# A three-layer GRU on graphs and a routed feed-forward on one Trainium2 core: the gated groups routed and placed in pairs

## The chip, the cores and the metric

The kernel runs on one core of one Trainium2 chip. Its five engines each follow their own list of instructions and wait for each other on semaphores: TensorE (PE; PEld are its weight loads), VectorE (DVE), ScalarE (ACT), GpSimd (POOL) and SyncE (SP). Transfers run beside them on 16 DMA engines. The metric is the device time of one execution in microseconds (us), lower is better.

## The reference

```python
A = (adj != 0)                              # 64 graphs of 128 nodes, 128 channels
h = layernorm(x)
for i in range(3):                          # GRU on the graph
    m = h @ weight[i];  aggr = A^T m
    h = gru_cell(aggr, h, w_ih, w_hh, b_ih, b_hh)
x = x + h
xf = layernorm(x)                           # 8192 tokens
H = gelu(xf @ W1 + b1)                      # 128 -> 512, exact gelu
probs = softmax(H @ Wg + bg)                # 8 experts
assign = argmax(probs)
out = x + probs[assign] * (H @ Wd[assign] + bd[assign])
```

## The kernel before, in words

The 64 graphs are 16 groups of four (512 columns). Every order is written out by hand: each engine has its own block with the same step numbers.

**Opening and GRU steps.** 48 units (four groups in flight, three layers each), one per step. A unit needs its rows in a high and a low half, since a product of fp32 precision is made of three matmuls (`three`, L481 to L483). For units of the first layer VectorE makes the low half of unit 0 (L1026), GpSimd that of all others (`first_rows_low`, L363), and TensorE's `neighbours` (L517, L518) waits for it.

**Gate steps** (`gate_step` on each engine, s = 0 to 18). For group s TensorE transposes the rows (`turned`, L607, one step ahead), makes the hidden layer in four chunks in four banks (`hidden`), which ScalarE empties with gelu (L907); for group s-1 it makes the gate's logits (L650). VectorE *routes* group s-2: it turns the logits (L1179), finds the winning expert and writes a one-hot tile `oh`. TensorE counts with five small matmuls into bank `pF` how many earlier tokens chose each expert (the *ranks*, L668, L671), semaphore `g_rk`. VectorE *places* group s-3: from the ranks and a running `base` it makes the row number of each token (`pos`, last instruction L1222), and the softmax gives its probability. GpSimd waits for both, then sends the group's four graphs of 128 rows by four indirect DMAs to the buffer `sorted_rows` in HBM, sorted by expert (L448). TensorE's four hidden banks are one set, so the next group's chunk waits for ScalarE's gelu of the last, and that for TensorE's signal `g_w1`.

**Tables.** After the ranks of eight groups VectorE computes which expert each of the first 24 slots of 128 rows has (`full_blocks_counted`, `full_blocks_placed`). `table(1)`, after TensorE's step 11, turns that by matmuls into one row of bank `pT`, VectorE copies it to `tables` (`tabled`, L1263, semaphore `tab_ok`), and TensorE's next transposes, which write `pT` too, wait for it. `table(2)` does the same for the rest, among the expert steps.

**Expert steps.** 18 slot groups (71 slots): SyncE loads sorted rows, TensorE makes the hidden layer again and the product with the slot's expert (L712), VectorE adds bias, multiplies by the probability and adds the residual (L1374, L1378), GpSimd scatters each slot's rows to the output (L459). After steps 9, 12 and 15 GpSimd drains its queue (`RETIRE`, L475). The last three slot groups use three banks in turn (`YB`).

## Time and profile before

| | us |
|---|---|
| median of 3 runs | 567.49 (566.56 to 571.98) |
| the profiled execution, its own time | 569.5 |
| its span | 567.8 |
| TensorE / weight loads busy | 511.8 / 418.8 |
| VectorE / ScalarE / GpSimd busy | 370.2 / 331.4 / 376.9 |
| mean granted clock of TensorE | 0.947 |

A step of the GRU and a gate step follow each other closely on TensorE; from about 288 us on the program is in the gate steps, from about 412 us in the expert steps. "remote" or "another core or an unknown queue" as a releaser means that the profile does not show what the engine waited for; "issue" that the engine itself was late.

### The profile page before, as it was taken

Reading aid. Unit: us, or ns where it says so; the run is one execution under the profiler, and the core shown is the slowest. Engines: PE = TensorE matmul, PEld = TensorE weight load, DVE = VectorE, ACT = ScalarE, POOL = GpSimd, SP = SyncE. Lnnn points to the kernel's source line nnn. Section 1 sums busy time; section 2 is a strip of 40 time slices with the busy share of each in tenths; the row PEclk is TensorE's granted clock in tenths of the full one; section 3 lists DMA queues with packets and bytes.
Section 4 is the critical chain, followed back from the end, with each engine's and each line's share of the span. In section 5 each row is a group of like instructions: output and inputs, shape, how many; then the busy total and the mean of one; then the engine's idle time right before and its main releaser. Section 6 shows DMA issues by size and latency. Waiting matters only on the chain.

```text
span 567.8 us, 10433 instructions
## 1 busy us (share of the span) xinstructions
PE 511.8 (90%) x3249; PEld 418.8 (74%) x3249; DVE 370.2 (65%) x1154; ACT 331.4 (58%) x594; POOL 376.9 (66%) x373
## 2 busy tenths in 40 slices
PE   8899999999999999999999689686795999798794
PEld 4678888888888888888877457363584998696684
DVE  5768687798888878897798456454662544353452
ACT  3867986779776897678778357253432442442430
POOL 3579977799798997988756555543555446335545
PEclk9999999999999999999999888787897999799978
DMA  8794000000000000000000111133211322221100
GB/s 224 228 275 119 1 0 1 1 1 2 0 2 1 1 1 2 0 1 0 1 2 15 40 45 35 39 80 81 59 49 62 91 77 81 61 58 45 38 29 21
DMA packets 37317, 26.50 MB, mean 47 GB/s; under 512 B 6140, under 2 KB 33920, under 8 KB 37264
## 3 DMA queue, kind: packets, MB, share of 16 engines
q1 hardware_dynamic: 31344, 16.91, 11.1%
q0 software_dynamic: 4320, 8.53, 4.4%
q8 instruction: 28, 0.46, 0.4%
q10 hardware_dynamic: 1600, 0.40, 0.3%
q14 instruction: 25, 0.20, 0.2%
HBM read 16.69 MB, written 9.59 MB: 46 GB/s over the span
## 4 chain that ended last, share of the span: by engine, by line
PE 76%; issue 7%; DVE 5%; another core or an unknown queue 4%; ACT 3%; POOL 3%; DMA 1%; POOLq 1%; DVEq 0%; ACTq 0%
PE bank L481 17%; PE bank L483 17%; PE bank L482 16%; PE bank L712 8%; PE bank L518 4%; PE bank L504 3%; PE bank L517 3%; PE bank L650 3%; ACT adj_i L907 2%; POOL out_dram L459 2%; PE bank L607 1%; PE bank L698 1%; PE bank L567 1%; DMA xrow<-in_x_dram 1%
## 5 line engine op out<-in xcount | busy, mean ns | idle before, releaser
L907 ACT ACTIVATE adj_i<-bank,b1c 128x512 f32<-128x512 f32 (+1 forms) x136 | 88.4, 686 | 139.3 <-PE bank L483 84.3
L459 POOL DMA_INDIRECT out_dram<-cand,home x71 | 70.3, 991 | 69.5 <-DVE cand L1378 40.8
L448 POOL DMA_INDIRECT sorted_rows<-xrow,pos x64 | 62.0, 968 | 57.5 <-issue 49.9
L369 POOL TENSOR_TENSOR diff<-hT,n_sb 128x512 f32<-128x512 f32 x48 | 76.4, 1592 | 11.4 <-ACT n_sb L814 11.4
L712 PE MATMUL bank<-wd_sb,adj_i 128*128 x568 | 71.1, 283 | 8.3 <-issue 8.3
L712 PEld LDWEIGHTS bank<-wd_sb,adj_i 128*128 128x128 f32 x568 | 69.0, 199 | 9.2 <-issue 9.1
L481 PE MATMUL bank<-hT_hi,w_hi 128*128 128x512 f32 (+1 forms) x136 | 63.1, 464 | 5.4 <-issue 3.0
L371 POOL TENSOR_TENSOR diff<-z_sb,diff 128x512 f32<-128x512 f32 x48 | 63.4, 1321 | 3.8
L481 PE MATMUL bank<-ag_hi,wf_hi 128*128 128x512 f32 x144 | 61.0, 423 | 0.2 <-DVE ag_lo L1064 0.2
L481 PE MATMUL bank<-hT_hi,whh_hi 128*128 128x512 f32 x144 | 59.5, 413 | 0.6 <-issue 0.6
L483 PE MATMUL bank<-hT_hi,w_lo 128*128 128x512 f32 (+1 forms) x136 | 58.2, 428 | 1.5 <-issue 1.4
L482 PE MATMUL bank<-hT_lo,w_hi 128*128 128x512 f32 (+1 forms) x136 | 58.0, 427 | 1.2 <-issue 1.0
L483 PE MATMUL bank<-hT_hi,whh_lo 128*128 128x512 f32 x144 | 57.9, 402 | 0.0
L482 PE MATMUL bank<-hT_lo,whh_hi 128*128 128x512 f32 x144 | 57.8, 402 | 0.0
L483 PE MATMUL bank<-ag_hi,wf_lo 128*128 128x512 f32 x144 | 57.1, 397 | 0.0
L482 PE MATMUL bank<-ag_lo,wf_hi 128*128 128x512 f32 x144 | 56.7, 394 | 0.0
L388 POOL TENSOR_TENSOR hT_lo<-hT,hT_hi 128x512 fp32r<-128x512 f32 x32 | 41.4, 1294 | 11.7 <-ACT hT_hi L893 11.7
L518 PE MATMUL bank<-A,hn_lo 128*128 128x128 f32 x192 | 45.5, 275 | 0.0
L517 PE MATMUL bank<-A,hn_hi 128*128 128x128 f32 x192 | 43.1, 263 | 1.9 <-POOL hn_lo L363 1.7
L1374 DVE TENSOR_TENSOR r_sb<-bank,bd_bc 128x128 f32<-128x128 f32 x71 | 19.2, 288 | 38.0 <-remote 27.3
L1077 DVE TENSOR_TENSOR hT<-n_sb,diff 128x512 f32<-128x512 f32 x48 | 41.5, 864 | 0.4 <-POOL diff L371 0.4
L1064 DVE TENSOR_TENSOR ag_lo<-bank,ag_hi 128x512 fp32r<-128x512 f32 x48 | 33.0, 687 | 13.3 <-ACT ag_hi L853 13.2
(176 smaller groups left out, 1153.2 us busy)
## 6 DMA issues: line engine op xcount, KB each, us to landing
adj_i<-sorted_rows SPq DMA_DIRECT2D x71, 66.0 KB
xrow<-in_x_dram SPq DMA_DIRECT2D x16, 256.0 KB, 3.7
adj_i<-in_adj_dram SPq DMA_DIRECT2D x16, 256.0 KB, 4.0
out_dram<-cand,home POOLq DMA_INDIRECT x71
sorted_rows<-xrow,pos POOLq DMA_INDIRECT x64
sorted_rows<-padrow SPq DMA_DIRECT2D x9, 66.0 KB
bd_bc<-in_L_ffn_bd_dram SPq DMA_DIRECT2D x1, 512.0 KB, 4.4
w1raw<-in_L_ffn_W_dram SPq DMA_DIRECT2D x1, 256.0 KB, 4.3
```

What stands on the lines that cost most here:

```text
L369: nc.gpsimd.tensor_tensor(diff[:, b, :], hT[:, g, :], n_sb[:, b, :], ALU.subtract).then_inc(diff_ok, 1)
L371: nc.gpsimd.tensor_tensor(diff[:, b, :], z_sb[:, g, :], diff[:, b, :], ALU.mult).then_inc(zd_ok, 1)
L448: nc.gpsimd.indirect_dma_start(out=sorted_rows, out_offset=bass.IndirectOffsetOnAxis(ap=pos[:, g, j:j + 1], axis=0), in_=xrow[:, g * GR + ...
L459: nc.gpsimd.indirect_dma_start(out=h_out, out_offset=bass.IndirectOffsetOnAxis(ap=home[:, s - 1, j:j + 1], axis=0), in_=yo[:, b, j, :], in ...
L481: nc.tensor.matmul(o, w_hi, x_hi, start=start, stop=False)
L482: nc.tensor.matmul(o, w_hi, x_lo, start=False, stop=False)
L483: return nc.tensor.matmul(o, w_lo, x_hi, start=False, stop=stop)
L517: nc.tensor.matmul(pAG[:, c], hn_hi[:, u % 2, c], A[:, u % QUAD, c], start=True, stop=False)
L518: last = nc.tensor.matmul(pAG[:, c], hn_lo[:, u % 2, c], A[:, u % QUAD, c], start=False, stop=True)
L712: last = nc.tensor.matmul(o, HT[:, sg % 2, k, j * P:(j + 1) * P], wd_sb[:, bass.ds(at + k * P, P)], start=(k == 0), stop=(k == KC - 1))
L907: nc.scalar.activation(HT[:, hb, k, 0:n], HB[k][:, 0:n], ACT.Gelu, bias=b1c[:, k:k + 1]).then_inc(done, 1)
L1077: tt(hT[:, u % QUAD, :], n_sb[:, u % 2, :], diff[:, u % 2, :], ALU.add).then_inc(h_ok, 1)
```

## The change

Gated groups are handled two at a time. Their tiles are twice as wide (`DUO` = 8 graphs), and one bank of logits holds both groups. VectorE routes a pair at odd steps from 3 on (`routed`), TensorE makes the pair's ranks with nine matmuls at the end of the same step, and VectorE places the pair at the next, even step (`placed`); GpSimd then issues eight scatters in a row. Besides: GpSimd drains after expert steps 6 and 12 instead of 9, 12 and 15; the low half of unit 2 is made by VectorE in its opening step 1, behind its adjacency; the tables go to columns 128 to 511 of the ranks' bank `pF` instead of `pT`, the first one inside TensorE's step 12 behind its transposes, and what waits for the copy is no longer the transposes but the ranks of step 13; the three banks of the last slots are taken in another order.

```diff
-        RETIRE = (9, 12, 15)
+        RETIRE = (6, 12)
+        DVE_LOW = (0, 2)
...
+        def routed(s):
+
+            return (s - 3) // 2 if s % 2 and inside(s - 3, GROUPS) else None
+
+        def placed(s):
+
+            return (s - 4) // 2 if s % 2 == 0 and inside(s - 4, GROUPS) else None
...
                 if s == 1:
                     row_scale(3)
-                    first_rows_low(2)
                     old_state(0)
...
-                g = s - 3
                 if s == 3:
                     row_scales(QUADS - 1)
-                if inside(g, GROUPS):
-
-                    if g == 0:
+                q = placed(s)
+                if q is not None:
+
+                    if q == 0:
                         pool.wait_ge(g_tok, 1)
-                    pool.wait_ge(g_prob, g + 1)
-                    pool.wait_ge(g_pos, g + 1)
+                    pool.wait_ge(g_prob, q + 1)
+                    pool.wait_ge(g_pos, q + 1)
                     settle(pool)
-                    for j in range(GR):
+                    for j in range(DUO):
                         nc.gpsimd.indirect_dma_start(
-                            out=sorted_rows, out_offset=bass.IndirectOffsetOnAxis(ap=pos[:, g, j:j + 1], axis=0),
-                            in_=xrow[:, g * GR + j, :], in_offset=None).then_inc(g_early if g < EARLY else g_late, 16)
+                            out=sorted_rows, out_offset=bass.IndirectOffsetOnAxis(ap=pos[:, q, j:j + 1], axis=0),
+                            in_=xrow[:, q * DUO + j, :], in_offset=None).then_inc(
+                                g_early if q * DUO < EARLY * GR else g_late, 16)
...
-                    pe.wait_ge(x0lo_ok, made("first", u) - 1) if u else pe.wait_ge(x0lo_first, 1)
+                    if u in DVE_LOW:
+                        pe.wait_ge(x0lo_first, DVE_LOW.index(u) + 1)
+                    else:
+                        pe.wait_ge(x0lo_ok, made("first", u) - sum(v < u for v in DVE_LOW))
...
-                if g == EARLY + 5:
-                    pe.wait_ge(tab_ok, 1)
...
+                if s == EARLY + 4:
+                    table(1)
...
-                    hold(pe, g_lgT, s - 2)
+                    pair, half_of = (s - 1) // 2, slice((s - 1) % 2 * P, ((s - 1) % 2 + 1) * P)
+                    hold(pe, g_lgT, pair - 1)
...
+                    pe.wait_ge(g_oh, q + 1)
+                    hold(pe, g_pos, q)
+                    if s == EARLY + 5:
+                        pe.wait_ge(tab_ok, 1)
...
+                    for j in range(1, DUO + 1):
+                        last = nc.tensor.matmul(pF[:, j * E:(DUO + 1) * E], ones[:],
+                                                oh[:, q % 2, 0:DUO + 1 - j, :].rearrange("p g e -> p (g e)"),
+                                                start=False, stop=(j == DUO))
...
+                hold(pe, tab_ok, n - 1)
                 if n == 1:
-                    pe.wait_ge(g_xlo, EARLY + 5)
-                else:
-                    pe.wait_ge(e_xlo, 4)
+                    pe.wait_ge(g_pos, RANKED)
                 for k in range(3):
-                    last = nc.tensor.matmul(pT[0:1, k * P:(k + 1) * P], tab[:, k:k + 1], ident[:],
+                    last = nc.tensor.matmul(TAB[:, k * P:(k + 1) * P], tab[:, k:k + 1], ident[:],
...
-                if sg == 4:
-                    pe.wait_ge(tab_ok, 2)
...
-            YB = (pF, pX, pAG)
+            YB = (pF, pAG, pX)
...
+            def rows_low_early(u):
+                dve.wait_ge(x0hi_ok, made("first", u))
+                tt(hn_lo[:, u % 2, :], xn[:, u % QUAD, :], hn_hi[:, u % 2, :].bitcast(fp32), ALU.subtract).then_inc(x0lo_first, 1)
...
+                    rows_low_early(2)
...
+                if route is not None:
+                    q, b = route, route % 2
+                    lg = lg4[:, b, :, :]
+                    dve.wait_ge(g_lg, 2 * q + 2)
+                    nc.vector.transpose(lgT[:, b, :, :].rearrange("p g c -> p (g c)"), LG[b][:, 0:2 * P]).then_inc(g_lgT, 1)
+                    dve.wait_ge(g_lgT, q + 1)
+                    tt(lg, lgT[:, b, :, 0:E], bg_bc[:].unsqueeze(1).to_broadcast([P, DUO, E]), ALU.add).then_inc(g_lg4, 1)
+                    dve.wait_ge(g_lg4, q + 1)
                     red(mx[:, b, :], lg, AX.X, ALU.max).then_inc(g_dve, 1)
+                    dve.wait_ge(g_dve, q * ROUTE + 1)
+                    tt(sh[:, b, :, :], lg, mx[:, b, :].unsqueeze(2).to_broadcast([P, DUO, E]),
                        ALU.subtract).then_inc(g_sh, 1)
+                    dve.wait_ge(g_sh, q + 1)
                     stt(mt[:, b, :, :], sh[:, b, :, :], 0.0, rev[:], ALU.is_ge, ALU.mult).then_inc(g_dve, 1)
+                    dve.wait_ge(g_dve, q * ROUTE + 2)
+                    red(mv8[:, b, :], mt[:, b, :, :], AX.X, ALU.max).then_inc(g_dve, 1)
+                    dve.wait_ge(g_dve, q * ROUTE + 3)
+                    tt(oh[:, b, 0:DUO, :], mt[:, b, :, :], mv8[:, b, :].unsqueeze(2).to_broadcast([P, DUO, E]),
+                       ALU.is_equal).then_inc(g_oh, 1)
+                if place is not None:
+                    q, d = place, place % 2
+                    dve.wait_ge(g_rk, q + 1)
+                    tt(rk[:, d, :, :], pF[:, 0:DUO * E].rearrange("p (g e) -> p g e", g=DUO),
+                       base[:].unsqueeze(1).to_broadcast([P, DUO, E]), ALU.add).then_inc(g_place, 1)
+                    dve.wait_ge(g_place, q * PLACE + 1)
+                    tt(base[:], pF[:, DUO * E:(DUO + 1) * E], base[:], ALU.add).then_inc(g_base, 1)
+                    tt(rk[:, d, :, :], rk[:, d, :, :], oh[:, d, 0:DUO, :], ALU.mult).then_inc(g_place, 1)
+                    dve.wait_ge(g_place, q * PLACE + 2)
                     red(posf[:, d, :], rk[:, d, :, :], AX.X, ALU.add).then_inc(g_place, 1)
+                    dve.wait_ge(g_place, q * PLACE + 3)
+                    nc.vector.tensor_copy(pos[:, q, :], posf[:, d, :]).then_inc(g_pos, 1)
+                if s == EARLY + 4:
+                    tabled(0, EARLY_SLOTS, 1)
```

VectorE, where a gated group in the middle is routed and the one before it placed; before the change every step has this piece (`lgT` to `oh` route, `rk`, `base`, `posf`, `pos` place, `hT_lo` is the next group's low half):

```order
L1179 STREAM_TRANSPOSE lgT<-bank 128x128
L1188 TENSOR_TENSOR rk<-bank,base 128x32
L1192 TENSOR_TENSOR lg<-lgT,bg_bc 128x32
L1195 TENSOR_REDUCE mx<-lg 128x4
L1201 TENSOR_TENSOR sh<-lg,mx 128x32
L1205 TENSOR_TENSOR base<-bank,base 128x8
L1206 TENSOR_TENSOR rk<-rk,oh 128x32
L1211 SCALAR_TENSOR_TENSOR mt<-sh,rev 128x32
L1214 TENSOR_REDUCE posf<-rk 128x4
L1219 TENSOR_REDUCE mv<-mt 128x4
L1222 CAST pos<-posf 128x4
L1227 TENSOR_TENSOR oh<-mt,mv 128x32
```

VectorE at the same place with the change, the placement of an even step and the routing of the odd step behind it:

```order
L1215 TENSOR_TENSOR rk<-bank,base 128x64
L1218 TENSOR_TENSOR base<-bank,base 128x8
L1219 TENSOR_TENSOR rk<-rk,oh 128x64
L1221 TENSOR_REDUCE posf<-rk 128x8
L1223 CAST pos<-posf 128x8
L1019 TENSOR_TENSOR hT_lo<-bank,hT_hi 128x512
L1014 SCALAR_TENSOR_TENSOR xn<-xrow 128x128 x2
L1197 STREAM_TRANSPOSE lgT<-bank 128x256
L1199 TENSOR_TENSOR lg<-lgT,bg_bc 128x64
L1201 TENSOR_REDUCE mx<-lg 128x8
L1203 TENSOR_TENSOR sh<-lg,mx 128x64
L1206 SCALAR_TENSOR_TENSOR mt<-sh,rev 128x64
```

Placement and routing no longer alternate instruction by instruction; each stands alone in every second step.

TensorE around the first table, before the change (ranks, table, transposes of the next group, its hidden layer):

```order
L668 MATMUL bank<-oh,before 128x40
L671 MATMUL bank<-oh,ones 128x32
L671 MATMUL bank<-oh,ones 128x24
L671 MATMUL bank<-oh,ones 128x16
L671 MATMUL bank<-oh,ones 128x8
L684 MATMUL bank<-ident,tab 1x128 x3
L607 MATMUL bank<-ident,xn 128x128 x4
L481 MATMUL bank<-hT_hi,w_hi 128x512
```

TensorE at the same place with the change:

```order
L687 MATMUL bank<-oh,before 128x72
L690 MATMUL bank<-oh,ones 128x64
L690 MATMUL bank<-oh,ones 128x56
L690 MATMUL bank<-oh,ones 128x48
L690 MATMUL bank<-oh,ones 128x40
L690 MATMUL bank<-oh,ones 128x32
L690 MATMUL bank<-oh,ones 128x24
L690 MATMUL bank<-oh,ones 128x16
L690 MATMUL bank<-oh,ones 128x8
L621 MATMUL bank<-ident,xn 128x128 x4
L702 MATMUL bank<-ident,tab 1x128 x3
L494 MATMUL bank<-hT_hi,w_hi 128x512
```

The table has moved behind the transposes, and one set of nine rank matmuls stands for two sets of five.

## Rows read from the trace of the kernel before

**Rows 1.** The page, part 2: TensorE's granted clock in 40 slices.
```profile
PEclk9999999999999999999999888787897999799978
```

**Rows 2.** The chain of waits, first gated steps: start, duration, engine, tile, line.
```profile
303.79 0.49 PE bank L607 x4
308.42 0.49 PE bank L607 x4
```

**Rows 3.** Timeline of GpSimd, routing scatters: start us, us, instruction, [idle before <-releaser].
```profile
307.33 1.25 POOL L448 DMA_INDIRECT sorted_rows<-xrow,pos  x1 [0.80 <-issue]
...
321.38 0.95 POOL L448 DMA_INDIRECT sorted_rows<-xrow,pos  x1 [3.86 <-issue]
...
327.83 0.96 POOL L448 DMA_INDIRECT sorted_rows<-xrow,pos  x1 [1.71 <-issue]
...
341.97 0.96 POOL L448 DMA_INDIRECT sorted_rows<-xrow,pos  x1 [3.70 <-issue]
...
349.84 0.95 POOL L448 DMA_INDIRECT sorted_rows<-xrow,pos  x1 [3.12 <-issue]
...
363.83 0.96 POOL L448 DMA_INDIRECT sorted_rows<-xrow,pos  x1 [4.10 <-issue]
...
380.65 0.96 POOL L448 DMA_INDIRECT sorted_rows<-xrow,pos  x1 [3.47 <-issue]
...
397.77 0.96 POOL L448 DMA_INDIRECT sorted_rows<-xrow,pos  x1 [7.34 <-DVE pos L1222]
...
405.79 0.96 POOL L448 DMA_INDIRECT sorted_rows<-xrow,pos  x1 [3.17 <-issue]
...
421.29 0.96 POOL L448 DMA_INDIRECT sorted_rows<-xrow,pos  x1 [5.24 <-issue]
```

**Rows 4.** The scatters' line: min/median/max ns, first and last start.
```profile
L448 POOL DMA_INDIRECT sorted_rows<-xrow,pos x64: 952/958/1246, 307.3 to 425.1; - x64
```

**Rows 5.** Timeline of ScalarE around the first long run of scatters.
```profile
309.72 1.33 ACT L907 ACTIVATE adj_i<-bank,b1c 128x512 f32<-128x512 f32 x2 [0.17 <-PE bank L483]
318.97 1.26 ACT L907 ACTIVATE adj_i<-bank,b1c 128x512 f32<-128x512 f32 x2 [7.04 <-remote]
```

**Rows 6.** Windows: busy us (count) of PE, PEld, DVE, ACT, POOL; clock, DMA, GB/s.
```profile
312.00:314.00 2.00, 2.00 (x16) 1.54 (x16) 1.37 (x7) 0.00 (x0) 1.43 (x2) 1.00 0.10 34
```

**Rows 7.** Timeline of TensorE, the transposes behind the first table.
```profile
370.28 0.63 PE L607 MATMUL bank<-ident,xn 128*128 128x128 f32 x4 [3.12 <-DVE tables L1263]
```

**Rows 8.** Timeline of VectorE, the last instruction of a placement.
```profile
379.67 0.17 DVE L1222 CAST pos<-posf 128x4 uint32<-128x4 f32 x1
```

**Rows 9.** Timeline of GpSimd, output scatters of groups 6, 7, 9, 10 and 12.
```profile
466.39 0.98 POOL L459 DMA_INDIRECT out_dram<-cand,home  x1 [2.80 <-DVE cand L1378]
...
473.88 0.98 POOL L459 DMA_INDIRECT out_dram<-cand,home  x1 [2.55 <-DVE cand L1378]
...
491.13 0.98 POOL L459 DMA_INDIRECT out_dram<-cand,home  x1 [7.26 <-DVE cand L1378]
...
505.14 0.98 POOL L459 DMA_INDIRECT out_dram<-cand,home  x1 [9.16 <-issue]
...
518.61 0.98 POOL L459 DMA_INDIRECT out_dram<-cand,home  x1 [3.36 <-DVE cand L1378]
```

**Rows 10.** The drains' line, in the queue of GpSimd: min/median/max ns.
```profile
L475 POOLq DRAIN  x3: 4963/5047/11122, 493.1 to 543.9; - x3
```

**Rows 11.** Timeline of TensorE, unit 2 of the opening.
```profile
25.37 0.30 PE L517 MATMUL bank<-A,hn_hi 128*128 128x128 f32 x1 [1.69 <-POOL hn_lo L363]
```

**Rows 12.** Windows, the same columns as rows 6, behind that wait.
```profile
26.50:29.90 3.40, 3.40 (x9) 2.67 (x9) 1.03 (x3) 3.36 (x7) 1.28 (x1) 0.51 0.73 211
```

**Rows 13.** Timeline of VectorE, unit 0's low half; unit 2's turned rows.
```profile
9.26 0.69 DVE L1026 TENSOR_TENSOR hn_lo<-xn,hn_hi 128x512 fp32r<-128x512 f32 x1 [0.36 <-ACT hn_hi L835]
...
24.89 0.68 DVE L1013 TENSOR_TENSOR hT_lo<-bank,hT_hi 128x512 fp32r<-128x512 f32 x1
```

**Rows 14.** The page, part 3: TensorE's instruction queue (packets, MB, share).
```profile
q8 instruction: 28, 0.46, 0.4%
```

149 lines of the change are left out of this document (46 added, 103 removed).

## The prediction

> **What bounds the kernel now.** I read the page's clock row first. TensorE's granted clock reads 9 in each of the first 22 of 40 slices and falls below that again and again from the 23rd on [rows 1]; 22 slices of 14.2 us are 312 us, early in the gate steps. So the GRU steps are TensorE at its own pace, and the stage the change works in is one where TensorE is not fed.
>
> How far it is not fed comes from two rows of the chain. Two neighbouring gate steps begin their transposes at 303.79 and 308.42 [rows 2]: an undisturbed step takes 4.63. The stage takes much more. GpSimd's scatters of the first gated group begin at 307.33 and those of the sixteenth at 421.29 [rows 3]: 113.96 us for 15 groups, 7.60 a group. Some 3 us a group are lost.
>
> Where they go is in the spacing of GpSimd's scatters. One takes 0.96 [rows 4] and 0.30 more until the next, so 1.265, four take 5.1 and eight 10.1. Since an undisturbed TensorE step (4.63) is shorter than four scatters (5.1), GpSimd falls behind, and the scatters of two groups run into one. The ten rows shown are starts of such runs (one more, of four, at 372.32, is left out): runs of eight begin at 307.33, 327.83, 349.84, 380.65 and 405.79 (in two of them with a gap under 1 us in the middle), runs of four at 321.38, 341.97, 363.83, 372.32 and 397.77.
>
> What a long run does is seen on ScalarE. In the run from 307.33 to 317.5 its last gelu that starts in time is at 309.72; the next starts at 318.97 after 7.04 of waiting on something the profile can't name [rows 5], 1.4 after the run's end. Yet TensorE was busy for all of 312 to 314 [rows 6]. So what ScalarE lacked was the signal of work that TensorE had done: from about 3 us after the start of a run of scatters, TensorE's signals are not seen until about 1 us after its end. A run of four holds them for some 2 to 3 us, which an engine one chunk ahead survives; a run of eight holds them for 8 and starves everybody. This is my reading, not a row; the change tests it, since it makes **every** run one of eight.
>
> **The change part by part.** The sum is made against the profiled execution (569.5, span 567.8); the median of the runs is 567.49, 2.0 less.
>
> *Low half of unit 2.* TensorE waits 1.69 for GpSimd's [rows 11], behind which 3.4 us run at the low clock [rows 12], 1.7 of them lost. VectorE makes the same half in 0.69 [rows 13] behind its adjacency and has it before TensorE's transposes end. But the next matmuls also need the low half of the turned rows, which VectorE starts at 24.89 and ends at 25.5 [rows 13]; without the wait TensorE would be at 24.6, with it 25.6 instead of 26.3. So 0.7 is sure, and if the shorter idle keeps the clock up, 1.7 more. I take **-1.5**, ends -0.6 and -2.4. VectorE's reset behind it comes at most 0.1 later.
>
> *The pairs, as runs of scatters.* The number of scatters stays 64 and each is as long. From the start of a run of eight to the start of the next run it took 14.05, 14.14, 13.99, 17.12 and 15.50 [rows 3], mean 14.96, so 7.48 a group; from a run of four 6.45, 7.87, 8.49, 8.33 and 8.02, mean 7.83. These contain the starving, the low clock behind it and the work of two steps or one. The first pair is placed at step 4. TensorE starts that at 308.42 [rows 2]; five small VectorE instructions of about 0.2 and the 0.98 from the last of a placement (379.67, [rows 8]) to GpSimd's start (380.65, [rows 3]) make 2.1, so 310.5. Seven runs later, at 14.96, the last pair's run starts at 415.2, where the last group's started at 421.29: **-6.1**. Ends: seven at 13.99 give 408.4, -12.9; seven at 17.12 give 430.3, +9.0. The mean is nearest, since the five runs span the stage.
>
> *The seam.* The last run before was four scatters of group 15 and four of the first output slots. Now it is eight and four, and TensorE waits for its end either way: four more scatters, 4 x 1.265 = **+5.1**; no less than 0 if the output scatters come so late that they don't join.
>
> *The first table.* Before, TensorE's transposes wait 3.12 for VectorE's copy [rows 7]; this lies inside a run of four (363.83). Now the transposes don't wait, but the table inside step 12 waits for that step's placement, 1.1 after the step's start where the transposes end at 0.5, and is then read by VectorE ahead of its next low half. I take 0.6 and 0.8 for the three matmuls. The runs of eight, with which I priced the pairs, hold no table, so this is **+1.4**, ends 0 and +3.1. The second table likewise no longer blocks transposes; it still comes behind the seam, and I give it nothing.
>
> *Drains.* The drain behind output step 9 is the long one of the three (11.1, the others 5.0, [rows 10]); GpSimd's next scatter comes after 9.16 of idle, and three output steps take 491.13 to 518.61 = 27.5 instead of three times the 7.49 of 466.39 to 473.88 [rows 9]: 5.0 lost. Step 6's drain now meets 88 scatters since the start instead of 100 and should be as long, so that loss moves rather than goes. Step 7's run of eight (473.88 to 491.13, 17.25 for two steps, 2.3 over) may be spared, as the drain shifts GpSimd anyway. The drain behind 15 lay within a wait for VectorE. **-1**, ends -4.5 and +4.5 (the drain at 12 now closes 24 scatters instead of 12 and could be long too).
>
> *Costed at nothing.* Eight matmuls fewer of 2463 rows and 144 fewer small VectorE instructions: VectorE is waiting in every starved stretch, and its low half comes as early as before in even steps. If that cover went, its routing of 256 columns would delay the ranks by half a microsecond a pair. The new order of the last three banks is a change of name, and its cover is GpSimd's own line of last scatters.
>
> Sum: -1.5 - 6.1 + 5.1 + 1.4 - 1 = **-2.1**, so 567.4 for such an execution and **565.4** beside the median shown. The gain of fewer runs is given back at the seam.
>
> **The rivals.** One percent is 5.7 us; below that I call it no change.
>
> *Every pair pays the longest run (slower).* Of the 9.3 us of TensorE's two steps between placements 2.1 have passed when the run starts. The hold bites before the second group's hidden layer is emptied, and TensorE gets through some 5. The remaining 2.2 begin at the run's end plus one, 10.9; the low clock adds 2.2, placement and GpSimd's start 2.1: 17.4 a pair, close to the 17.12 seen once. It decides at one point: whether the next pair's ranks are done before the hold. Before, groups were placed singly, so at the end of a run one placement was often already due, and this speaks for the rival; three of five runs at 14 speak against. The seven runs then end at +9.0 instead of -6.1: **580.5**.
>
> *Every pair as the best run (faster).* With nine instead of ten small matmuls, no placement between routing instructions and no table wait, all runs may take 13.99, and the drain at 6 falls where the seam's backlog would have been: 6.8 and 3.5 less than the forecast, **555**.
>
> *The stalls are TensorE's own instruction stream, not GpSimd's scatters.* The instruction queue moved 28 blocks [rows 14], one for each 20 us or so. Then pairing changes nothing about them, and what stays is the opening and the table's wait: -1.5 - 3.1, so **562.9**. Against it: GpSimd's run and ScalarE's wait end together. The Trainium skill, page "Runtime: NRT & Kernel Launch", section "Instruction fetch mechanics", says that such 16 KiB blocks are fetched ahead and mostly hidden; by that this rival has no stalls to explain and falls.
>
> **How the numbers follow.** Forecast 0.34 (its own range 558 to 572, from the ends of the pair term over three or four of the seven runs), the longest run 0.28, the best run 0.26, the instruction stream 0.12. The range over all reaches from just below the best case to the longest: **553 to 581**. Faster by over 1%: all of the best run, a third of the forecast's span and little else, 0.38. Slower: the longest run and a remainder of the drains, 0.29. Same: 0.33.
>
> **What would show it.** In the new trace each GpSimd run in the gate steps should have eight scatters; the spacing of their starts says which case it is (14 to 15.5, or over 17). ScalarE's waits should number one per pair, ending 1 to 1.6 after a run. The run at the seam should have twelve scatters. TensorE's wait at unit 2 should be under 1 and the low clock behind it gone or not. The first table's wait should be near 0.6. The forecast is wrong if runs of eight no longer starve ScalarE, or if something else (VectorE's routing, output scatters that wait for a drain) sets the pace.

## The result: 2.3% slower

The changed kernel takes 578.34 us (median of 4 runs, 575.19 to 581.64) beside 567.02 for the kernel before (4 runs, 562.5 to 571.98) on the same chip: ratio 1.0229, 95% interval 1.0167 to 1.0291. The profiled execution took 580.23, its span is 578.5 (before: 569.5 and 567.8). The forecast was 565.4. The measurement lies 2.2 us below the rival "every pair pays the longest run" (580.5). Here and below a time is the median of all runs and a ratio that of the fast runs alone (for the split pairs' 0.9776 two of the four), so the two need not divide out.

Where it went is read from GpSimd's timeline. First the starts of its runs of scatters in the changed kernel, the last two of them output scatters of steps 2 and 3 (columns as in [rows 3]):

```profile
309.15 1.25 POOL L460 DMA_INDIRECT sorted_rows<-xrow,pos  x1 [5.26 <-issue]
...
322.75 0.96 POOL L460 DMA_INDIRECT sorted_rows<-xrow,pos  x1 [3.52 <-issue]
...
336.34 0.96 POOL L460 DMA_INDIRECT sorted_rows<-xrow,pos  x1 [3.71 <-DVE pos L1223]
...
353.77 1.00 POOL L460 DMA_INDIRECT sorted_rows<-xrow,pos  x1 [7.63 <-DVE pos L1223]
...
370.68 0.96 POOL L460 DMA_INDIRECT sorted_rows<-xrow,pos  x1 [7.06 <-DVE pos L1223]
...
390.47 0.96 POOL L460 DMA_INDIRECT sorted_rows<-xrow,pos  x1 [9.84 <-DVE pos L1223]
...
408.87 0.96 POOL L460 DMA_INDIRECT sorted_rows<-xrow,pos  x1 [8.61 <-DVE pos L1223]
...
428.21 0.95 POOL L460 DMA_INDIRECT sorted_rows<-xrow,pos  x1 [9.54 <-issue]
...
444.84 0.98 POOL L472 DMA_INDIRECT out_dram<-cand,home  x1 [1.68 <-DVE cand L1371]
...
457.51 0.98 POOL L472 DMA_INDIRECT out_dram<-cand,home  x1 [7.82 <-DVE cand L1371]
```

Each of the eight runs in the gate steps has eight scatters, and behind the last of them four of the first output step follow at once: the run of twelve. The starts are 13.60, 13.59, 17.43, 16.91, 19.79, 18.40 and 19.34 apart, 17.0 in the mean, where the forecast took 14.96. Of the ten starts in [rows 3] one waited for VectorE's positions (`pos`), now five of the seven behind the first do. Set against the prediction's terms, from the same starts (before: 307.33 and 421.29 in [rows 3], output step 3 at 443.30, last scatter at 564.92; after: last scatter at 575.13):

| stretch | before | after | change | forecast |
|---|---|---|---|---|
| first scatter | 307.33 | 309.15 | +1.8 | +1.7 |
| from there to the last run of the stage | 113.96 | 119.06 | +5.1 | -7.8 |
| from there to output step 3 (the seam) | 22.0 | 29.3 | +7.3 | +5.1 |
| from there to the last scatter | 121.6 | 117.6 | -4.0 | -1.0 |
| sum | | | +10.2 | -2.1 |

In the second row the forecast is its 104.7 for seven pairs less 113.96, and the table's 1.4. That row alone is 12.9 off, more than the 12.3 by which the sum misses.

How one pair comes to 17 us is seen in the run from 353.77 (timelines of ScalarE, VectorE and TensorE, in order of time; x26 and x3 are matmuls in one group):

```profile
359.50 0.69 ACT L921 ACTIVATE adj_i<-bank,b1c 128x512 f32<-128x512 f32 x1 [4.28 <-PE bank L496]
...
359.84 0.23 DVE L1210 TENSOR_TENSOR oh<-mt,mv 128x64 bf16<-128x64 f32 x1
...
361.67 1.92 PE L667 MATMUL bank<-adj_i,wg_sb 128*32 128x128 f32 x26 [3.51 <-ACT adj_i L921]
...
365.17 0.65 PE L667 MATMUL bank<-adj_i,wg_sb 128*32 128x128 f32 x3 [0.79 <-issue]
...
366.35 0.63 PE L495 MATMUL bank<-hT_lo,w_hi 128*128 128x512 f32 x1
...
368.43 0.21 PE L687 MATMUL bank<-oh,before 128*128 128x72 bf16 x1
...
369.70 0.17 DVE L1223 CAST pos<-posf 128x8 uint32<-128x8 f32 x1
```

The run lasts until 363.6. In TensorE's list the next pair's ranks stand behind the second step's logits and its last two hidden chunks. The logits are through 2.2 us after the run's end, and the chunks follow at the low clock (a matmul of 512 columns takes 0.63, where it takes 0.40 at the full one). Then ranks, positions and GpSimd's start follow in a row: 363.6 + 4.8 + 1.3 + 1.0 = 370.7. From the run's length (9.85) and this chain (7.1) come the 16.9. The one-hots that the ranks need were ready at 360.07; the 8.4 us until the ranks are the price of TensorE's order, and no run tried another.

In the next run, from 370.68 to 380.63, VectorE can't even route before the run has ended. It waits for the pair's logits, the last of which TensorE made between 372.36 and 373.44 (VectorE's timeline):

```profile
382.17 0.45 DVE L1197 STREAM_TRANSPOSE lgT<-bank 128x256 f32<-128x256 f32 x1 [9.95 <-remote]
```

That one takes 19.79 to the next start, the longest of the seven.

TensorE's granted clock tells the same over the kernel (page, one digit per fortieth of the span; [rows 1] is its partner):

```profile
PEclk9999999999999999999999978777897899988998
```

The opening came as forecast. VectorE's new instruction is in time (its timeline):

```profile
22.79 0.69 DVE L1036 TENSOR_TENSOR hn_lo<-xn,hn_hi 128x512 fp32r<-128x512 f32 x1 [0.59 <-ACT hn_hi L849]
```

TensorE no longer waits for unit 2's low half, and the first hidden-state matmul of the next unit starts at 32.31, before at 34.14: 1.8 gained (TensorE's timeline, the first such matmul of unit 2 and of the one behind it):

```profile
25.64 0.47 PE L494 MATMUL bank<-hT_hi,whh_hi 128*128 128x512 f32 x1 [0.93 <-issue]
...
32.31 0.47 PE L494 MATMUL bank<-hT_hi,whh_hi 128*128 128x512 f32 x1 [0.28 <-issue]
```

The low clock behind the wait is gone: the window of [rows 12], its granted clock 1.00 where it was 0.51.

```profile
26.50:29.90 3.40, 3.40 (x16) 2.69 (x15) 1.03 (x2) 3.37 (x8) 0.39 (x2) 1.00 0.98 274
```

Where [rows 7] had a wait of 3.12, TensorE's timeline has the first table's matmuls, 0.71 + 0.81 = 1.5 where 1.4 was forecast:

```profile
370.02 0.81 PE L702 MATMUL bank<-ident,tab 128*1 128x128 f32 x6 [0.71 <-DVE pos L1223]
```

The drains' line, as in [rows 10], has the long one again, now behind output step 6:

```profile
L488 POOLq DRAIN  x2: 5461/8000/10540, 481.9 to 533.0; - x2
```

### The profile page after: what moved, and what is told of

It reads as the page before. It is cut to its first block, busy times and chain, and to the rows that moved or that the text cites. A ratio compares the mean times of both kernels' runs of the same rounds, so it can differ in the third digit from the quotient of the medians.

```text
span 578.5 us, 10235 instructions
## 1 busy us (share of the span) xinstructions
PE 511.6 (88%) x3241; PEld 420.3 (73%) x3241; DVE 361.7 (63%) x1019; ACT 330.9 (57%) x586; POOL 375.4 (65%) x372
## 3 DMA queue, kind: packets, MB, share of 16 engines
q1 hardware_dynamic: 31344, 16.91, 11.0%
## 4 chain that ended last, share of the span: by engine, by line
PE 76%; another core or an unknown queue 6%; DVE 5%; ACT 5%; issue 5%; POOL 1%; DVEq 1%; DMA 1%; POOLq 0%; ACTq 0%
PE bank L494 17%; PE bank L496 16%; PE bank L495 16%; PE bank L728 10%; PE bank L534 3%; PE bank L517 3%; PE bank L533 3%; PE bank L667 3%; ACT adj_i L921 3%; PE bank L621 1%; PE bank L583 1%; PE bank L714 1%; DVEq L207 1%; DMA xrow<-in_x_dram 1%
## 5 line engine op out<-in xcount | busy, mean ns | idle before, releaser
L728 PE MATMUL bank<-wd_sb,adj_i 128*128 x568 | 77.3, 291 | 17.5 <-issue 16.0
L728 PEld LDWEIGHTS bank<-wd_sb,adj_i 128*128 128x128 f32 x568 | 72.2, 205 | 21.9 <-issue 21.9
L384 POOL TENSOR_TENSOR diff<-z_sb,diff 128x512 f32<-128x512 f32 x48 | 64.6, 1347 | 3.8
L496 PE MATMUL bank<-hT_hi,w_lo 128*128 128x512 f32 (+1 forms) x136 | 56.9, 418 | 1.2 <-issue 1.2
L400 POOL TENSOR_TENSOR hT_lo<-hT,hT_hi 128x512 fp32r<-128x512 f32 x32 | 42.0, 1311 | 10.3 <-ACT hT_hi L907 10.1
L667 PE MATMUL bank<-adj_i,wg_sb 128*32 128x128 f32 x512 | 22.6, 312 | 26.1 <-ACT adj_i L921 24.6
```

The lines of the kernel that those rows point to most:

```text
L384: nc.gpsimd.tensor_tensor(diff[:, b, :], z_sb[:, g, :], diff[:, b, :], ALU.mult).then_inc(zd_ok, 1)
L400: nc.gpsimd.tensor_tensor(hT_lo[:, u % QUAD, :], hT[:, u % QUAD, :], hT_hi[:, u % QUAD, :].bitcast(fp32), ALU.subtract).then_inc(htlo_ok, 1)
L496: return nc.tensor.matmul(o, w_lo, x_hi, start=False, stop=stop)
L728: last = nc.tensor.matmul(o, HT[:, sg % 2, k, j * P:(j + 1) * P], wd_sb[:, bass.ds(at + k * P, P)], start=(k == 0), stop=(k == KC - 1))
```

## The experiments

Three theories were put up. **A, the length of the runs**: while GpSimd issues scatters back to back, TensorE's signals don't come through, and a run of eight starves the others. **B, the pairs' routing**: logits, one-hots, ranks and positions of two groups follow one another, so the placement is late whatever GpSimd does. **C, TensorE's instruction stream**, with the scatters only coinciding. The experiments ran on five chips; each ratio is to the kernel before on the same chip.

### Four that met a chip without the hold

Everything but the pairs (groups one at a time; opening, drains, tables of the change):

```diff
-        RETIRE = (9, 12, 15)
+        RETIRE = (6, 12)
+        DVE_LOW = (0, 2)
...
+        RANKED = EARLY + 2
+        TAB = pF[0:1, P:4 * P]
...
```

> The kernel before with everything of the change except the pairs: unit 2's low half on VectorE, drains at steps 6 and 12, both tables in the ranks' bank and the banks of the last three results in the new order. Groups are still routed, placed and scattered one at a time. Both theories of the loss (below) lie in the pairs, so both expect this kernel to be no slower than before: opening -1.8 (what the changed kernel's trace showed for the next unit's hidden-state matmuls, 32.31 against 34.14), tables between -1 and +1, drains between 0 and -4: 561 to 567, ratio 0.990 to 1.000. If it is slower than before by more than 3 us, the loss is not the pairs' and both theories fall.

The pairs with the opening and drains of before:

```diff
-        RETIRE = (6, 12)
-        DVE_LOW = (0, 2)
+        RETIRE = (9, 12, 15)
...
```

> The changed kernel with its opening and its drains as they were before (low half of unit 2 on GpSimd, drains at 9, 12 and 15): what is left is the pairs, with the tables' place that their code shares. If the parts add up, this is the change's 1.0229 less what the run of everything else gains: 1.025 to 1.035, 581 to 587. Spacing of the starts of GpSimd's runs of eight in the gate steps as in the changed kernel, 17.0 on average.

Single routing, scatters in eights:

```diff
-                if inside(g, GROUPS):
...
+                if inside(g, GROUPS) and g % 2:
...
-                    for j in range(GR):
...
+                    for h in (g - 1, g):
+                        for j in range(GR):
...
```

> The kernel before, routing and placing each gated group by itself as before, but GpSimd issues the scatters of two groups together at every second step, so that every run is one of eight; the pairs' routing isn't there. Theory A (the length of the runs: TensorE's signals are held while GpSimd issues scatters, and a run of eight starves the others): as slow as with pairs, starts of the runs 16 to 18 apart, 573 to 583. Theory B (the pairs' routing: what is late is the placement, since logits, one-hots, ranks and positions of two groups follow one another in a row only after the run has ended, where the single groups have a placement ready): the positions of the first group of two are long there, and only one group's are to be made, so starts 14 to 15.5 apart and 562 to 570.

The pair's eight split by a landing:

```diff
                     for j in range(DUO):
+                        if j == GR:
+                            early = q * DUO < EARLY * GR
+                            pool.wait_ge(g_early if early else g_late, (q * DUO + GR - (0 if early else EARLY * GR)) * 16)
```

> The changed kernel with a pause in each run of eight scatters: the fifth is issued only when the first four have landed (some 2 us). Routing and placement stay paired. Theory A: two runs of four with a pause in which TensorE's signals come through; ScalarE and VectorE lose at most some 2 us each time, so the starts of the pairs are 14 to 15 apart and the kernel takes 562 to 570. Theory B: the chain from logits to positions is as long as before and starts no sooner, so the starts stay 17 apart or more, 576 to 584.

Measured: 503.33, 509.13, 513.02 and 514.24 us, ratios 0.9963 (0.9948 to 0.9978), 1.0063 (1.0039 to 1.0087), 1.0135 (1.0083 to 1.0188) and 1.0176 (1.0147 to 1.0206), all beside a kernel before of **505.08**. Every number in us missed, because this chip runs the kernel before 62 us faster. The trace of "everything but the pairs" shows how: 64 scatters follow one another almost without a break for 84 us, and nobody is starved (all breaks over 0.6 in GpSimd's timeline of the 64):

```profile
305.47 1.25 POOL L450 DMA_INDIRECT sorted_rows<-xrow,pos  x1 [0.80 <-issue]
...
357.06 0.96 POOL L450 DMA_INDIRECT sorted_rows<-xrow,pos  x1 [0.77 <-issue]
...
385.41 0.96 POOL L450 DMA_INDIRECT sorted_rows<-xrow,pos  x1 [3.34 <-issue]
```

In the middle of it ScalarE's gelus wait 0.17 (its timeline):

```profile
335.61 1.33 ACT L909 ACTIVATE adj_i<-bank,b1c 128x512 f32<-128x512 f32 x2 [0.17 <-PE bank L485]
```

TensorE's 32 small weight loads of the logits go in 0.81 (its weight loads' timeline, two steps):

```profile
336.14 0.81 PEld L655 LDWEIGHTS bank<-adj_i,wg_sb 128*32 128x32 f32 x32 [0.37 <-issue]
340.77 0.81 PEld L655 LDWEIGHTS bank<-adj_i,wg_sb 128*32 128x32 f32 x32 [0.37 <-issue]
```

And the page's clock row has no low stretch:

```profile
PEclk9999999999999999999999999998999999999998
```

A step takes 4.63 there with scatters on (336.14 to 340.77), as [rows 2] has it without. So a scatter is not what stops TensorE; on the other chips something comes with it. Where nothing is held, GpSimd's own issue (1.265 a scatter) is the stage's pace, and what the pairs cost is that it starts later: the first scatter at 310.61 instead of 305.47 (1.8 of it the opening), and from there 10.4 a pair as against 10.3 for two groups. Between the theories these runs decide nothing: there is no hold to be explained on this chip.

### The change itself, twice more

> The changed kernel itself, unaltered, beside the kernel before. The first four experiments ran where the kernel before takes 505 us, not 567, and where ScalarE never waits long for TensorE in a run of scatters: the hold is absent there, so the result with its 1.0229 must be taken again under the same conditions. Where before takes 505: theory A (the hold) then has nothing to say; GpSimd's own 64 scatters at 1.265 are the stage's bound, and what the pairs cost is the later first run (step 4 instead of 3, one undisturbed step of 4.63 or one group's scatters of 5.06), less what the run of everything else gained (0.9963): 506 to 509, ratio 1.001 to 1.008. Where before takes 567: 1.02 again.

> The changed kernel itself again, beside the kernel before on the same chip as the two runs above, so that the split has its own partner: theory A expects it 1.01 to 1.03 where before takes 562 to 575, with starts of the pairs' runs 16.5 to 18.5 apart in the mean; 1.003 to 1.008 where before takes 505.

574.11 beside 569.98, ratio 1.0127 (1.0052 to 1.0203), and 581.32 beside 568.32, 1.0253 (1.0183 to 1.0323). Both chips hold the signals. The starts of the pairs' runs are 17.1 and 17.6 apart in the mean, with five waits for positions in each; the first two runs start 13.6 apart, the next follows after 15.0 and 15.6, and the last three after 19.1 to 20.5. The intervals of the three comparisons just overlap; the price of the change is 1.3 to 2.5%. The first lies under the 1.02 that was expected, but its interval reaches it; the second is in its range.

### The hold by itself

```diff
...
+            pool.wait_ge(g_h, 2)
+            for k in range(IDLE_RUN):
+                nc.gpsimd.indirect_dma_start(
+                    out=nowhere, out_offset=bass.IndirectOffsetOnAxis(ap=ids[:, k:k + 1].bitcast(u32), axis=0),
+                    in_=padrow[:], in_offset=None).then_inc(idle_out, 16)
             for s in range(3, GROUPS + 3):
```

> The kernel before with eight further scatters, issued together by GpSimd as soon as two of the first gate step's hidden chunks are emptied, long before the first real ones: they take constant rows to rows of their own in DRAM that nobody reads, and no engine waits for them before the end. They measure the hold by itself, with no routing and no placement near it. Theory A, if the hold is there: ScalarE's gelus stop 2 to 3 us after the first of the eight starts and go on 1 to 1.5 us after the last ends, one wait of 5 to 7 us, and the gate steps 0 to 2 take that much longer. Where the kernel before takes 505 (no hold): no wait of ScalarE above 1.5, steps of 4.6. Theory C (the stalls are TensorE's own instruction stream and not the scatters'): no wait here wherever it runs.

One execution, 576.0 us, so nothing is read from its time. The eight idle scatters run from 299.32 to 309.44. The 32 small matmuls of a step's logits otherwise take 1.1 together; here they take 6.2 (TensorE's timeline):

```profile
304.95 1.09 PE L658 MATMUL bank<-adj_i,wg_sb 128*32 128x128 f32 x25 [0.83 <-ACT adj_i L915]
306.50 0.30 PE L658 MATMUL bank<-adj_i,wg_sb 128*32 128x128 f32 x2 [0.47 <-issue]
307.92 0.31 PE L658 MATMUL bank<-adj_i,wg_sb 128*32 128x128 f32 x2 [1.12 <-issue]
309.37 0.44 PE L658 MATMUL bank<-adj_i,wg_sb 128*32 128x128 f32 x2 [1.13 <-issue]
310.78 0.37 PE L658 MATMUL bank<-adj_i,wg_sb 128*32 128x128 f32 x1 [0.97 <-issue]
```

ScalarE in the same run:

```profile
303.63 1.27 ACT L915 ACTIVATE adj_i<-bank,b1c 128x512 f32<-128x512 f32 x2 [2.51 <-PE bank L491]
...
308.01 0.69 ACT L915 ACTIVATE adj_i<-bank,b1c 128x512 f32<-128x512 f32 x1 [0.93 <-remote]
310.11 0.69 ACT L915 ACTIVATE adj_i<-bank,b1c 128x512 f32<-128x512 f32 x1 [1.41 <-remote]
```

These transfers wait for no group's routing or placement (VectorE does route and place beside them, from 302.91 to 306.52), and still TensorE's work reaches ScalarE late from 2 us after their start (the gelu at 303.63 had waited since 301.1), and its own small matmuls are stretched until 1.6 us after their end. That speaks for A and against B. C is gone in its plain form: the choking comes and goes with the scatters. The form was missed, though: not one wait of 5 to 7 us but five of 0.9 to 2.5, since signals dribble out rather than stop. It shows in the kernel before as well, in the run from 380.65 ([rows 3]), once one looks at the weight loads:

```profile
384.17 0.59 PEld L650 LDWEIGHTS bank<-adj_i,wg_sb 128*32 128x32 f32 x23 [0.37 <-issue]
384.92 0.11 PEld L650 LDWEIGHTS bank<-adj_i,wg_sb 128*32 128x32 f32 x1 [0.15 <-issue]
385.65 0.11 PEld L650 LDWEIGHTS bank<-adj_i,wg_sb 128*32 128x32 f32 x1 [0.63 <-issue]
386.38 0.11 PEld L650 LDWEIGHTS bank<-adj_i,wg_sb 128*32 128x32 f32 x1 [0.62 <-issue]
387.80 0.11 PEld L650 LDWEIGHTS bank<-adj_i,wg_sb 128*32 128x32 f32 x1 [1.31 <-issue]
389.22 0.13 PEld L650 LDWEIGHTS bank<-adj_i,wg_sb 128*32 128x32 f32 x1 [1.32 <-issue]
389.94 0.13 PEld L650 LDWEIGHTS bank<-adj_i,wg_sb 128*32 128x32 f32 x1 [0.59 <-issue]
```

23 loads go at full pace, as 25 of the matmuls do in the idle run. The steps between the starts of the next six are 0.73, 0.73, 1.42, 1.42 and 0.72: one or two times some 0.72 us.

### Drains alone

```diff
-        RETIRE = (9, 12, 15)
+        RETIRE = (6, 12)
```

> The kernel before with GpSimd's drains behind output steps 6 and 12 instead of 9, 12 and 15, nothing else. Each drain costs the wait for GpSimd's outstanding work if the scatters behind it are due; one drain less at 5 to 8 us each that lies partly on the path: ratio 0.990 to 1.000. If everything but the pairs gained 1.8 in this (0.9963) with the opening, the drains alone should be within 1 us of before.

564.05 beside 569.98: 0.9928 (0.9878 to 0.9979), by the ratio -4.1 us. Inside the range given, beyond its last sentence (within 1 us), which had leaned on the chip without the hold. The forecast's -1 was too small, its end of -4.5 held.

### Runs of four by a wait for landing, groups one at a time

```diff
+                    if g:
+                        early = g - 1 < EARLY
+                        pool.wait_ge(g_early if early else g_late, (g - (0 if early else EARLY)) * GR * 16)
                     settle(pool)
                     for j in range(GR):
```

> The kernel before, in which each group's four scatters are issued only when the four of the group before have landed, so that no two groups' scatters ever run into one. Theory A with the hold there (before at 567): the runs of eight go, ScalarE waits at most some 2 us per group, a group takes 6.5 to 7.3 instead of 7.6: 550 to 562. Without the hold (before at 505): GpSimd is the bound and gets a pause of 1.6 per group, 15 x 1.6 = 24 less what it was idle anyway; 515 to 528.

559.3 beside 569.98: **0.9847** (0.9779 to 0.9914). Starts 6.95 to 7.66 apart, from 305.93 to 412.66: 7.12 a group where it was 7.60. A pause of 2.2 to 2.9 in GpSimd's work makes the kernel faster, as theory A had it.

### The two that decide, where the signals are held

> Single routing and placement, scatters of two groups issued together, a second time, since the first time ran where the kernel before takes 505 and TensorE's signals aren't held. If this one runs where before takes 562 to 575: theory A (length of the runs) says starts of runs 16 to 18.5 apart and a time like the changed kernel's less its opening, ratio 1.01 to 1.03; theory B (the pairs' chain from logits to positions) says starts 14 to 15.5 apart, ratio 0.99 to 1.005. Where before takes 505 again: 1.0135 as measured.

> The changed kernel with the fifth scatter of a pair held until the first four have landed, a second time. Where before takes 562 to 575: theory A says that the pairs' starts are 14.0 to 15.5 apart and the ratio is 0.98 to 0.995 (the run in which every group waited for the one before to land gave 0.985 and 6.97 a group; opening and drains gain on top, the pairs' first run a step later loses 5); theory B says 17 or more apart and a ratio of 1.01 to 1.03. Where before takes 505 again: 1.018 as measured.

The same two kernels as the third and fourth above, now beside a before of 566.95. Scatters in eights with single routing: 587.02, **1.0333** (1.0266 to 1.0399), at least as slow as the change itself (1.0127 to 1.0253 on three others), which has the opening and the drains to its credit. The changed kernel with its eight split: 558.36, **0.9776** (0.969 to 0.9861; 0.984 when it was repeated on another chip, below). The first is a little over its range (1.01 to 1.03), the second better than its (0.98 to 0.995). Starts of the long runs of the first (GpSimd's timeline):

```profile
337.91 0.96 POOL L449 DMA_INDIRECT sorted_rows<-xrow,pos  x1 [4.22 <-issue]
...
355.64 0.96 POOL L449 DMA_INDIRECT sorted_rows<-xrow,pos  x1 [7.88 <-DVE pos L1223]
...
374.74 0.95 POOL L449 DMA_INDIRECT sorted_rows<-xrow,pos  x1 [9.19 <-DVE pos L1223]
...
394.59 0.96 POOL L449 DMA_INDIRECT sorted_rows<-xrow,pos  x1 [10.05 <-DVE pos L1223]
...
432.24 0.96 POOL L449 DMA_INDIRECT sorted_rows<-xrow,pos  x1 [9.85 <-DVE pos L1223]
```

The split, from its first scatter (the same view):

```profile
309.04 1.25 POOL L463 DMA_INDIRECT sorted_rows<-xrow,pos  x1 [5.27 <-issue]
...
315.67 0.96 POOL L463 DMA_INDIRECT sorted_rows<-xrow,pos  x1 [1.61 <-DMA sorted_rows<-xrow,pos]
...
320.72 0.95 POOL L463 DMA_INDIRECT sorted_rows<-xrow,pos  x1 [0.30 <-issue]
...
327.05 0.96 POOL L463 DMA_INDIRECT sorted_rows<-xrow,pos  x1 [1.58 <-DMA sorted_rows<-xrow,pos]
```

(309.85 to 432.24) / 7 = 17.5 a run without any paired routing, against the changed kernel's 17.0; (309.04 to 410.79) / 7 = 14.5 a pair with the paired routing and a pause of 1.6 to 2.3. One has the long runs without the pairs and loses, the other the pairs without the unbroken eight and gains: theory B falls, A stands. The split is not clean: 315.67 to 325.5 is again a run of eight, the second half of one pair and the first of the next, and so is the run from 342.82; from 354.22 on every run in the gate steps is of four, until the last, which the output scatters join.

### Everything but the pairs, without and with the wait for landing

> Everything of the change but the pairs, a second time. Where before takes 562 to 575: the drains alone gave 0.9928 there, the opening 1.8 us more, the tables 0 to 3 for them: ratio 0.980 to 0.993. The whole change gave 1.0127 and 1.0229 there, so the pairs alone would be worth +2 to +4 per cent. Where before takes 505 again: 0.996.

> Everything of the change but the pairs, and each group's four scatters wait until the four before have landed: the version that the runs so far point to where the hold is there. Where before takes 562 to 575: 0.985 for the wait alone, 0.993 for the drains alone, 1.8 us for the opening: if they add up 0.972 to 0.982, 551 to 558. Where before takes 505: the pause costs some 20 us of GpSimd, ratio 1.02 to 1.05.

On the same chip as the two above: 563.69, 0.9953 (0.9897 to 1.001), and 557.68, 0.984 (0.9795 to 0.9885). The first lies above the range given, its interval reaches it; opening (-1.8) and drains (-4.1) would have made 0.990. The second lies above its range too, though its interval reaches it: the wait alone had 0.9847 on another chip, and opening and drains on top of it show no further gain. Set beside the split pairs of the same chip (0.9776, 0.969 to 0.9861), single groups with the wait (0.984, 0.9795 to 0.9885) are not told apart: once the runs are broken, handling groups in pairs is not shown to gain anything.

### Fewer instructions in the same run

```diff
-                    for k in range(KC):
+                    for k in range(1):
...
-                                                    start=(k == 0), stop=(k == KC - 1), tile_position=(0, q * CT))
+                                                    start=True, stop=True, tile_position=(0, q * CT))
```

> The kernel before without three quarters of its gate logits' matmuls: only the first of the four chunks is multiplied by the gate's weights (the logits, and with them the routing, are not the reference's; every row is still scattered). TensorE issues 24 small matmuls and 24 weight loads fewer per gate step, 0.8 us of its 4.6. What is open is what a run of scatters holds. If TensorE's issue and signals leave one by one (in the traces they come at multiples of 0.71 us during a run), fewer instructions get through the same run sooner: the stalls shrink with their number, a group takes 5.5 to 6.5 instead of 7.6 and the kernel gains 18 to 35 us: ratio 0.94 to 0.97. If signals are simply shut off for the length of the run, only the 0.8 x 16 = 13 us at most are gained, and less since GpSimd waits for the same placement: ratio 0.975 to 1.0. Where before takes 505: GpSimd's scatters are the bound and nothing is gained, 0.99 to 1.0.

This kernel leaves out three of the four chunks of the logits, so its routing is not the reference's, and its rows go to other places. 558.85 beside 568.32: 0.984 (0.9777 to 0.9902), 9 us. Undisturbed, its steps are 3.97 (306.82 to 310.79) instead of 4.63, which for 16 steps is 10.6. So nothing of the stalls went with three quarters of the logits' instructions; behind a run of eight the next still starts 13.6 to 13.9 later, and ScalarE still waits (its timeline; the run before it was one of twelve, from 307.16 to 322.42):

```profile
324.40 1.26 ACT L907 ACTIVATE adj_i<-bank,b1c 128x512 f32<-128x512 f32 x2 [6.93 <-remote]
```

Its eight small weight loads a step all go at full pace, so the steps of 0.72 are gone and the stalls are not. The picture of a queue that lets TensorE's instructions out one by one, each costing the same, is not supported. What fits is a hold that lasts as long as the run does.

### The output steps too

```diff
+                    if s == 1:
+                        pool.wait_ge(g_late, (GROUPS - EARLY) * GR * 16)
+                    else:
+                        pool.wait_ge(e_out[(s - 2) % 2], landed(s - 2, 2))
                     for j in range(slots(s - 1)):
```

> The changed kernel with the fifth scatter of a pair held until the first four have landed (0.978 so far), and now also each output step's first scatter held until the scatters before it have landed, so that no run of eight or twelve is left at the seam and behind the drains. Theory A: the seam's run of twelve and the two or three output runs of eight cost 5 to 8 us each beyond two runs of four, and the landing wait costs nothing where the steps are 7.5 apart anyway: 6 to 14 us less, ratio 0.953 to 0.970. If the output steps' stalls have another cause, 0.975 to 0.985.

563.79 beside 568.32 (one of its ten executions took 2285.92): 0.991 (0.9872 to 0.9948), where the split alone had 0.9776 and 0.984 on two other chips. Outside both ranges. In the profiled executions (566.93 and 559.83) the gate steps are as in the split alone (last pair's start 410.61 against 410.79), and the loss lies in the output steps, whose last scatter starts at 561.5 against 554.8. With the wait these are 7.0 or more apart and can't catch up: 3.2 of the 6.7 are lost by output step 6, the rest behind the first drain, where the split alone issues two steps' scatters in a row. So there breaking the runs doesn't pay. Why they cost less than in the gate steps is not shown.

### A break that waits for a signal

```diff
                     for j in range(DUO):
+                        if j == GR:
+                            if s + 1 < GROUPS:
+                                pool.wait_ge(g_h, (s + 1) * KC + 1)
+                            else:
+                                pool.wait_ge(e_h, (s + 1 - GROUPS) * KC + 1)
```

> The changed kernel whose fifth scatter of a pair waits for a gelu instead of a landing: the first of the next step (in the last two pairs the first one of the next output step). Where nothing is held that gelu is there before the first four scatters are issued, so the wait costs nothing; where TensorE's signals are held in the run, it ends only when they have come through, and the break is as long as needed. Theory A, where before takes 562 to 575: as good as the split by landing (0.978) or better, 0.965 to 0.985, the second half starting 1.5 to 3 after the end of the first. Where before takes 505: 1.000 to 1.008, as the changed kernel, and not the 1.018 of the split by landing.

In everything but the pairs:

```diff
+                    pool.wait_ge(g_h, min(s * KC + 2, GROUPS * KC))
                     settle(pool)
```

> Everything of the change but the pairs, and each group's scatters wait for the second gelu of the step in which the group is placed. Theory A, where before takes 562 to 575: runs of four with a break only as long as TensorE's signals need, so 0.970 to 0.984, as the wait for landing (0.984) or better; if GpSimd falls behind, the gelu is there before the run ends, runs of eight come back, and it stays at 0.990 to 0.996 as without the wait. Where before takes 505: 0.995 to 1.000.

> The changed kernel with the fifth scatter of a pair held until the first four have landed, again, as the partner of the two kernels above on their chip: 0.970 to 0.986 where before takes 562 to 575, pairs' starts 14.0 to 16.0 apart; 1.018 where it takes 505.

On one chip, beside a before of 571.78: 569.24, 0.9937 (0.9894 to 0.9979); 572.16, 0.9976 (0.9917 to 1.0035); and the split by landing 562.43, **0.984** (0.9786 to 0.9894), starts 14.5 apart. The first missed its range. GpSimd's timeline of it:

```profile
331.17 0.96 POOL L465 DMA_INDIRECT sorted_rows<-xrow,pos  x1 [3.58 <-ACT adj_i L926]
...
345.40 0.96 POOL L465 DMA_INDIRECT sorted_rows<-xrow,pos  x1 [4.44 <-ACT adj_i L926]
```

The breaks that wait for the gelu are 3.6 to 4.5 (the last one 2.3), not 1.5 to 3: the gelu stands behind all that the hold delayed. In three of the eight pairs it was there already and the four ran on into eight (from 309.14, 352.95 and 382.75). The second is no faster than before and went its other way (0.990 to 0.996 was given for it; its interval reaches that): the gelu is often there already, and the next run is one of eight (from 305.73, 321.25 and 337.34, 15.5 and 16.1 apart). So a break that is tied to the starved engine comes too long or not at all; the one tied to the landing comes each time, 1.6 to 2.3 long. Whether the transfers in flight or the issuing of scatters does the holding is not told apart by this.

## Why the prediction was wrong, point by point

- **What bounds the kernel** (runs of scatters hold TensorE's signals): right, shown by the idle run, and by eights and splits. That it isn't the scatter alone, since one chip has none of it, nothing in the trace of before could tell.
- **Opening, -1.5**: right; 34.14 to 32.31 is -1.8, with the clock's share.
- **The pairs, -6.1: the step that failed.** The term took the mean over five runs of eight as they occurred before (14.96) and multiplied it by seven; it measured 17.0, so the stretch came out at +5.1. Each of those five was the first run or stood behind a run of four; none stood behind another run of eight. With several in a row only the first two take 13.6 in the changed kernel's trace; from the third on they take 16.9 to 19.8, since each run starts the moment the chain behind the one before ends, and TensorE has only the 3 us before the hold for work that feeds the next placement. How much of that work gets through differs from run to run (16.91 from 353.77 with the routing done in the run, 19.79 from 370.68 with it done behind). 17.12, the largest row of before, was the only one of the five behind which GpSimd waited for the positions, the state that the change makes the rule. The rival said so, with the right mechanism (run's end, rest of two steps, low clock, placement: 17.4 against 17.0), and was given 0.28. That its total came within 2.2 us is in part luck: it had all seven alike, its seam was 2.2 too cheap and its drains 3.0 too dear. Eights with single routing (17.5) show that the length of the runs did it.
- **The seam, +5.1**: measured +7.3, and the run of twelve was there; the 2.2 more were not taken apart.
- **First table, +1.4**: right within 0.1 at its place (0.71 + 0.81).
- **Drains, -1**: -4.0 for the output steps of the change, -4.1 (0.9928) alone; the drain behind output step 12 is followed by only 3.2 of idle time, as steps without a drain are, so it nearly vanished.
- **Eight matmuls and 144 VectorE instructions fewer, costed at nothing**: not seen in any stretch; eights with single routing lose as much without it.
- **The best run as a rival** (555): the splits (558.36, 562.43) got near it only with a pause that the change lacks. **The instruction stream** (562.9): excluded by the idle run, and by the chip without the hold, whose trace has the same 28 instruction blocks and none of the stalls. The Trainium skill, page "Runtime: NRT & Kernel Launch", section "Instruction fetch mechanics", has instruction blocks fetched ahead and mostly hidden; no stall here had to be explained by them.

## What to carry to other kernels

When a change makes one case of a pattern the only one, ask whether any row has that case following itself. Here none had, and the mean of its isolated cases said nothing of a row of them; the nearest row was the one in which the wait that the change brings (for the positions) already ended last. Where an engine's wait ends with a burst of GpSimd's scatters rather than with the producer's own record, look for the burst's length first: a pause of 2.2 us or a little more behind every fourth scatter made the kernel before 1.5% faster, and one of 1.6 to 2.3 in each pair turned the change from 1.3 to 2.5% slower into 1.6 to 2.2% faster than before; on the chip where nothing is held the split pairs are 1.8% slower than before. So for a mixed set of chips none of the versions is best everywhere: everything but the pairs was never measured slower than before (0.9963, 0.9953), the split pairs beat it where signals are held (0.9776 against 0.9953 on one chip, the intervals apart), and single groups with the same kind of pause do as well there (0.984).

## What the runs showed of the hardware that was not expected

- Chips differ: the same kernel before takes 505.08 on one and 567 to 572 on the others. The first scatter of everything but the pairs starts at 305.47 on the one and 305.58 on another, so all of it lies in the stages with scatters, and in the low clock that the idle time brings (mean granted clock 0.993 against 0.93 to 0.96). A scatter takes 0.96 on both kinds, and in the split pairs four have landed as soon on both (breaks of 1.58 and up). What sets the two kinds of chip, or of placement on them, apart stays open; nothing here could vary it.
- During a long run of scatters on the held chips what TensorE has done reaches ScalarE and VectorE only after the run (waits of 8.22 and 9.95 in the run from 370.68), or bit by bit. VectorE's own instructions keep their pace once they have their input: seven of the routing go from 358.07 to 360.07, in the run from 353.77.
- In some of these runs TensorE's small weight loads come in two parts: 23 in 0.59 us, then the rest at one or two times 0.72 us. With eight of them in a step none is spaced so, and the stalls stay (0.984). What path is shared was not shown.
